# Mixture-of-experts kernel: the two transfers that fill the spare rows are sent in iterations 2 and 3, where iteration 6 sent both

## What is computed

```python
x = x + _L0_gnn_ref(_layernorm(x, axis=-1), adj, ...)
x = x + _L0_ffn_ref(_layernorm(x, axis=-1), ...)
# in _L0_ffn_ref
top_vals, top_idx = jax.lax.top_k(logits, K)          # K = 2 of E = 8
w = jax.nn.softmax(top_vals, axis=-1)
for e in range(E):
    h = jax.nn.gelu(jnp.einsum('bsd,dh->bsh', xn, W1[e]) + b1[e], approximate=False)
    y_e = jnp.einsum('bsh,hd->bsd', h, W2[e]) + b2[e]
    y = y + y_e * w_full[..., e, None]
```

## Time and profile before

| | us |
|---|---|
| median of 3 runs | 621.6 |
| lowest, highest | 621.08, 629.53 |
| the profiled execution | 620.77 |
| its span | 619.0 |
| PE busy in it | 588.4 |

### The profile page before, as it was taken

One profiled execution on the slowest core, in us unless ns is written; L12 is line 12 of the kernel. 1 busy time (PEld: TensorE's weight loads), 2 busy tenths in 40 slices (PEclk: granted clock), 3 DMA queues, 4 the chain that ended last, 5 costly groups with the idle time before them and its releaser, 6 DMA issues. The chain is left out here.

```text
span 619.0 us, 12907 instructions
## 1 busy us (share of the span) xinstructions
PE 588.4 (95%) x3936; PEld 515.5 (83%) x3936; DVE 493.0 (80%) x2046; ACT 369.8 (60%) x733; POOL 337.8 (55%) x249
## 2 busy tenths in 40 slices
PE   8999999999999999999999999999999998999990
PEld 6787778686879797979798989898989887999890
DVE  7978898898899898989898989888888865744330
ACT  5654547365758584948484848585766645554450
POOL 2000505133458655857778575767685845555765
PEclk9999999999999999999999999999999999999996
DMA  8519131325566996575666676566655866666853
GB/s 297 202 57 327 51 107 57 111 66 177 142 173 147 309 274 184 139 196 130 175 152 164 166 172 163 140 156 182 151 161 149 225 143 176 149 158 155 226 90 42
DMA packets 85860, 99.72 MB, mean 161 GB/s; under 512 B 7520, under 2 KB 62560, under 8 KB 85472
## 3 DMA queue, kind: packets, MB, share of 16 engines
q1 hardware_dynamic: 64064, 82.37, 42.4%
q0 software_dynamic: 21728, 16.53, 16.7%
HBM read 74.95 MB, written 30.39 MB: 170 GB/s over the span
## 5 line engine op out<-in xcount | busy, mean ns | idle before, releaser
L1043 POOL DMA_INDIRECT routed<-row,at_u x112 | 129.0, 1152 | 143.2 <-DVE at_u L1253 110.9
L1008 POOL DMA_INDIRECT out<-y_t,xt x88 | 146.3, 1662 | 95.5 <-DMA out<-y_t,xt 58.6
L569 PE MATMUL C<-cv_h,w_hi 128*128 128x256 f32 (+1 forms) x432 | 128.9, 298 | 2.9 <-ACT tz L921 1.5
L570 PE MATMUL C<-cv_l,w_hi 128*128 128x256 f32 (+1 forms) x432 | 123.4, 286 | 0.0
L571 PE MATMUL C<-cv_h,w_lo 128*128 128x256 f32 (+1 forms) x432 | 123.3, 285 | 0.0
L569 PEld LDWEIGHTS C<-cv_h,w_hi 128*128 128x128 f32 x432 | 81.7, 189 | 6.5 <-issue 2.8
L570 PEld LDWEIGHTS C<-cv_l,w_hi 128*128 128x128 f32 x432 | 81.4, 189 | 1.0
L571 PEld LDWEIGHTS C<-cv_h,w_lo 128*128 128x128 f32 x432 | 81.5, 189 | 0.7
L748 PE MATMUL G<-ex,msg_t 128*128 128x512 f32 x128 | 58.2, 597 | 1.7 <-ACT gh L940 1.7
L650 PE MATMUL Y<-w_t,ge 128*128 128x128 f32 x424 | 55.8, 274 | 0.0
L650 PEld LDWEIGHTS Y<-w_t,ge 128*128 128x128 f32 x424 | 51.7, 191 | 3.1 <-issue 2.6
(11 more groups left out here) (275 smaller groups left out, 1629.6 us busy)
## 6 DMA issues: line engine op xcount, KB each, us to landing
w_t<-w_all SPq DMA_DIRECT2D x63, 392.0 KB, 3.8
adj<-adj_t SPq DMA_DIRECT2D x16, 1024.0 KB, 5.8
xt<-routed SPq DMA_DIRECT2D x63, 144.0 KB, 2.3
wd<-w_all SPq DMA_DIRECT2D x11, 392.0 KB, 4.5
x_ln<-x SPq DMA_DIRECT2D x16, 256.0 KB, 2.9
x_res<-x_t SPq DMA_DIRECT2D x16, 256.0 KB, 6.1
out<-x SPq DMA_DIRECT2D x15, 256.0 KB
w_all<-w_s SPq DMA_DIRECT2D x1, 3136.0 KB, 10.3
```

The costliest lines, as they stand in the source:

```text
L569: pe.matmul(psum, hi(w), rhs_h, start=start, stop=False)
L570: pe.matmul(psum, hi(w), rhs_l, start=False, stop=False)
L1008: nc.gpsimd.indirect_dma_start(out=out, out_offset=bass.IndirectOffsetOnAxis(ap=xt[j][:, t, R_ID:R_ID + 1].bitcast(U32), axis=0), in_=y_t[ ...
L1043: nc.gpsimd.indirect_dma_start(out=routed, out_offset=bass.IndirectOffsetOnAxis(ap=ats_u[d % 2][:, n:n + 1], axis=0), in_=rows[d % 2][:, n ...
```

## The change

The transfer to `routed` is issued at the end of SP's iteration 2 and the one to `out` at the end of iteration 3. Both stood at the end of iteration 6. The wait on `pads_stored` in iteration 4 now asks for all three fills issued up to then. No other instruction changes.

```diff
                 if g == FIRST - 1:
                     sp.wait_ge(w12_stored, 16)
-                    sp.wait_ge(pads_stored, 16)
+                    sp.wait_ge(pads_stored, 48)
                 if FIRST - 1 <= g < GRAPHS - 1:
                     chosen[:] = [choice(g % 2, j) for j in range(SLOTS)]
                     for i in range(2):
                         sp.wait_ge(rows_out[i], 16 * NT * TOP * ((g - i) // 2))
                     for j in range(2):
                         batch_load(g + 1, j)
-                if g == FIRST + 1:
-
+                if g == 2:
                     sp.dma_start(routed[DUMMY + TAKEN:, :], pads[TAKEN:, :]).then_inc(pads_stored, 16)
+                if g == 3:
                     sp.dma_start(out[TOKENS + TAKEN:, :], pads[TAKEN:, 0:P]).then_inc(pads_stored, 16)
```

## The result

The changed kernel takes 616.53 us (median of 20 runs, 614.72 to 620.81), and the kernel before, in 20 runs as well, 622.43 us (620.03 to 631.02). The ratio is 0.9917, with a 95% interval of 0.9897 to 0.9937: faster by 0.8%, some 5 to 6 us, where 0.6 us had been forecast. Every ratio in this document leaves out executions more than 1.5% above the fastest of their kernel, so it can differ from the ratio of the two medians. The profiled execution took 616.99 us with a span of 615.2 us.

A forecast was written before the change was run, and what follows sets the result against it. PE was taken to bound the kernel (busy 588.4 of 619.0 us). Span 619.0 - 0.57 = 618.4, with 1.77 around it 620.2; for the median, 621.6 - 0.6 = 621.0 us, range 619.0 to 624.0.

The forecast's parts named there:

- What the two transfers cost PE where they run, 0.57 us: Iteration 6 to 7: period 32.48 us against 31.91 undisturbed, from tile 2's late rows; moving the transfers gains 0.57 us.
- Iterations 2 and 3 pay nothing: Each takes one added transfer; `x_res`, SP's next issue and POOL's scatters were expected to cost 0.
- the slower rival: Iterations 2 and 3: `x_res` lands late, DVE stalls; 0.1 + 2.9 us at most, less 0.57, so 624.0 us; chance 0.06.
- The wait in iteration 4: SP's wait at 138.8 us, now including both transfers, ends at once with 13 us to spare; cost 0.
- SP and POOL have idle time in iteration 7; an earlier finish there buys nothing: Iteration 7, after the transfers: freeing SP and POOL earlier adds nothing, so no more than 0.57 us can come.
- The last part: 487 to 619 us: released by PE's and DVE's results, so it begins and should end 0.57 us earlier.
- The adds can only follow PE's tiles: Last part: argument, with a 3.45 us gap, against the lost-gain rival (621.6 us, chance 0.10) that POOL has saved-up work.
- The larger gain: Rival: the 5.17 us issue disturbs more, for instance POOL's adds come late; another 0.5 us, so 620.5 us; chance 0.04.

The follow-up runs named there:

- LANDED 8: Kernel before with LANDED = 8 in place of 6, so last-part tile loads wait for adds eight tiles back, not six: 643.68 us, ratio 1.008.
- the pair side by side on chip B: Kernel before and changed kernel, with no further edit, timed and profiled again together on the second chip: 650.97 and 629.82 us, ratio 0.975.

## Why the prediction was wrong

The time predicted, 621.0 us with a range of 619.0 to 624.0, missed the 616.53 measured.

- *What the two transfers cost PE where they run, 0.57 us*: right. The load of tile 2 is issued at 220.02 in 0.37 us, PE has no wait from iteration 6 to 14, and the period is 31.91.
- *Iterations 2 and 3 pay nothing*: right. Periods and phases of these iterations are the same to 0.1 us, the DMA share is 0.49 and 0.51 as forecast, and DVE has no wait for `x_res`. The bound of 3.0 us for the slower rival was not needed. SP's issue of `x_res` in iteration 2 took 1.53 us in place of 0.51, which nobody waits for.
- *The wait in iteration 4*: right, no delay.
- *"SP and POOL have idle time in iteration 7; an earlier finish there buys nothing"*: this is the step that failed. POOL's idle time in iteration 7 of the kernel before was its wait for its own adds to land (5.8 us in two waits), which is part of its work and can't be used up, and the gaps of 0.30 us between two issues. What it has to spare is only its wait for DVE, 1.03 us, and in the kernel before even that row is gone from iteration 7 on. The busy share of POOL, 55%, says nothing of this. Holding POOL for 7 us brought the loss back without the transfers, and holding the others made the last part short (147.34 us) with the transfers in place.
- *The last part "begins 0.57 us earlier and should end so"*: wrong by 5.58 us, for the same reason. It was said to be released by PE's and DVE's results. It is POOL's chain of 38 adds that runs to the end, and its start had been late by 5.62 us.
- *"The adds can only follow PE's tiles"*, with the gap of 3.45 us before the add at 602.72 as evidence, was a misreading. The chain has eight gaps of 2.4 to 3.5 us in either kernel, of which the earlier trace rows show one. With LANDED 8, where PE's last matmul comes 5.2 us earlier, there are eight as well, and the chain is no faster. At each tile POOL waits for its own earlier adds as well as for the tile's result, so a gap is no sign that POOL has no work saved up.
- *The larger gain* named the right mechanism, adds that come late and catch up slowly, at a chance of 0.04 and a size of 0.5 us. The 5 us went beyond any case that it had priced. The evidence put against it, a next period of 31.91 us, was of PE. PE's period says nothing of a backlog on another engine as long as its buffers cover it. One look at POOL's place beside the mark in iterations 5, 6 and 8 would have shown 2, 2 and 9 us.

Shown by the runs, in one profiled execution of each: POOL's lateness is enough to cause the loss of the last part, its end is enough to stop it, and of the two transfers it is the one to `routed`, in long pieces, that starts it. Argued only: that the long pieces work by holding the DMA engines of the indirect transfers, and that the extra time in the loop on chip B comes of the lateness. Open: what ACT waits for there, why 2 us grow to 7, and why POOL slipped by itself in iteration 12 in two executions.

## What to carry to other kernels

When a burst delays an engine that is off the critical path, follow that engine's distance from a fixed mark through the later iterations, and not only the bound engine's period: in a loop where its true spare time (waits for others, without waits for its own results) is about 1 us in 32, a delay of 2 us can grow, last to the end and be paid there. Put bulk transfers where the indirect transfers have whole microseconds to spare, here before the expert tiles start. If they have to go into a tight loop, short pieces or parts are worth a try: here both left the iterations that held them undisturbed, though in both profiles POOL slipped later.

## What the runs showed of the hardware that was not expected

- Two transfers of nearly the same size act differently on the landings of indirect adds: beside 2,160 KB in pieces of 46,080 bytes POOL waited 2.3 us longer for one, beside 1,920 KB in pieces of 512 bytes not at all, nor beside the 2,160 KB in pieces of 512 and 64 bytes.
- The price of a late phase is not fixed: 5.6 us, all of it in the last part, in the first pair of profiles; 17.9 us, 14.1 of them in the loop, in the pair side by side on chip B.
- A stall of PE of 4.67 us was followed by 4.8 us at the lower of its two clock levels (granted clock 0.50), so that it cost 7.2 us in all.
